# Work moved into the joints between stages, and the picking one-hot as one fused vector operation, in a two-layer graph network kernel

## The reference, cut to what matters

```python
h = relu(layernorm(x))
agg = segment_sum(h[src] * edge_weight[:, None], dst)       # over incoming edges
x = x + agg @ W_neigh + b_neigh + h @ W_self.T
h = relu(layernorm(x))                                      # not used by the second layer's result
s, m, c = segment_sum(attr, src), segment_max(attr, src), count(src)
u = [s, where(c > 0, m, 0), s / max(c, 1), u0]
x = x + relu(u @ W1 + b1) @ W2 + b2
```

## Time and profile before

| | us |
|---|---|
| median of 3 runs | 1644.15 |
| lowest, highest | 1643.24, 1649.29 |
| the profiled execution | 1640.22 |
| its span, first to last instruction | 1638.5 |
| busy in the span: PE, DVE, ACT, POOL | 986.9, 1323.9, 727.7, 1254.9 |

### The profile page before, as it was taken

How to read it: one execution, slowest core, us unless ns; L and a number is a source line. 1 busy time by engine, 2 the same in 40 slices (tenths; PEclk the granted TensorE clock), 3 DMA queues, 4 the chain that set the end, 5 groups by cost and what they waited for, 6 DMA issues and landing times. The chain is left out here.

```text
span 1638.5 us, 39257 instructions
## 1 busy us (share of the span) xinstructions
PE 986.9 (60%) x13658; PEld 839.9 (51%) x13659; DVE 1323.9 (81%) x3122; ACT 727.7 (44%) x1864; POOL 1254.9 (77%) x1506
## 2 busy tenths in 40 slices
PE   3356666666656102333333333359999999999995
PEld 2245555555555101323332233348878888888884
DVE  6689999999999104766766775659999999999995
ACT  2268888888874001221222222214444444444442
POOL 7777777776777777777777777458888888888882
PEclk9567787887876555555565555559999999999998
DMA  9955555555554103444434332259999999999996
GB/s 300 162 125 125 117 117 125 122 126 117 117 117 117 35 14 85 118 114 108 108 99 105 98 81 75 88 141 195 208 205 212 208 208 210 207 208 210 205 210 62
DMA packets 507051, 229.55 MB, mean 140 GB/s; under 512 B 472141, under 2 KB 479565, under 8 KB 506173
## 3 DMA queue, kind: packets, MB, share of 16 engines
q0 software_dynamic: 148560, 98.39, 36.4%
q1 hardware_dynamic: 356558, 118.63, 33.8%
q10 hardware_dynamic: 1728, 9.94, 1.5%
HBM read 138.46 MB, written 88.33 MB: 138 GB/s over the span
## 5 line engine op out<-in xcount | busy, mean ns | idle before, releaser
L851 POOL DMA_INDIRECT xg_all<-in_x_dram,idx_src x391 | 397.0, 1015 | 120.2 <-issue 118.5
L857 POOL DMA_INDIRECT by_win<-rows,idx_win x391 | 389.4, 996 | 130.1 <-issue 129.5
L1186 PE MATMUL ps<-ident,h 128*128 128x128 f32 x588 | 138.1, 380 | 283.4 <-DVE h L1000 207.6
L1272 ACT ACTIVATE sq<-xc 128x512 f32<-128x512 f32 x147 | 92.6, 630 | 474.6 <-DVE xc L963 473.0
L1186 PEld LDWEIGHTS ps<-ident,h 128*128 128x128 f32 x588 | 93.4, 196 | 303.0 <-DVE h L1000 220.7
L952 DVE TENSOR_REDUCE stat<-xg_all 128x8 f32<-128x512 f32 x49 | 33.4, 682 | 233.0 <-DMA xg_all<-in_x_dram,idx_src 232.9
L1414 POOL DMA_DIRECT2D rows<-flag_d x392 | 197.0, 539 | 3.5 <-issue 3.5
L1290 ACT ACTIVATE h<-xc,stat 128x64 f32<-128x64 f32 x784 | 196.2, 332 | 0.0
L1425 POOL DMA_DIRECT2D out_dram<-rows x97 | 162.6, 1676 | 28.6 <-ACT rows L1616 21.7
L1570 PE MATMUL ps<-w_sb,arena 128*96 128x64 f32 x1568 | 156.5, 254 | 0.0
L1570 PEld LDWEIGHTS ps<-w_sb,arena 128*96 128x96 f32 x1568 | 142.9, 167 | 22.7 <-issue 22.7
(11 more groups left out here) (212 smaller groups left out, 2635.9 us busy)
## 6 DMA issues: line engine op xcount, KB each, us to landing
rows<-message SPq DMA_DIRECT2D x784, 36.4 KB, 3.6
rows<-flag_d POOLq DMA_DIRECT2D x392, 72.0 KB, 4.2
out_dram<-rows POOLq DMA_DIRECT2D x97, 256.0 KB, 6.2
message<-m_row SPq DMA_DIRECT2D x48, 388.0 KB, 2.4
arena<-in_x_dram SPq DMA_DIRECT2D x70, 256.0 KB, 3.6
out_dram<-arena SPq DMA_DIRECT2D x70, 256.0 KB, 2.9
zeros<-slot_d POOLq DMA_DIRECT2D x98, 144.0 KB, 4.1
by_win<-zeros ACTq DMA_DIRECT2D x12, 808.5 KB
```

The source lines that it names most:

```text
L851: nc.gpsimd.indirect_dma_start(out=xg[g % RX][:, t % GT, :], out_offset=None, in_=x, in_offset=bass.IndirectOffsetOnAxis(ap=idx_src[:, t:t ...
L857: nc.gpsimd.indirect_dma_start(out=by_win, out_offset=bass.IndirectOffsetOnAxis(ap=idx_win[0:parts, t:t + 1], axis=0), in_=rows[0:parts, t ...
L1186: last = nc.tensor.transpose(hT_of[n % 2][:, P * k:P * k + P], h[n % 2][:, 2 * k:2 * k + 2, :].rearrange("p a c -> p (a c)"), ident[:, :])
L1272: nc.scalar.activation(sq[:, :, :], xc[n % 2][:, :, :], ACT.Square).then_inc(ln["squared"], 1)
```

## The change

Its parts:

- *Start.* SP issues the main src load first, ahead of its wait for the pads. POOL clears only the columns from FT on of five tables. Gathers of full tiles read `src_i` directly; `idx_src` is one column, for the tail tile, and POOL waits for it only before the gathers of group 8 on.
- *First block, tail.* DVE makes the bias rows after edge steps 10 and 11, the counts after 12. After the last gather POOL makes a table `node_n`, 8 x 128 columns with 0 to 1023, and issues the loads of window groups 0 to 3. The last steps have an order of their own: DVE keeps the steps up to LAST-2 before it sums the last one.
- *Window block.* The loads of groups 0 to 3, the bias rows and PE's wait for them are gone. `picks` is one scalar_tensor_tensor: (key - 1024 g) == node_n.
- *Last block.* The counts are gone.

The tiles of the window block are laid out anew: loads, pick, node_n and the bias rows in `rows`, the rest in `arena`.

```diff
-        idx_src = sb("idx_src", [P, NT], U32)
+        idx_src = sb("idx_src", [P, 1], U32)
...
+                sp.dma_start(src_i[:, 0:FT], src[0:FT * P].rearrange("(p t) -> p t", p=P)).then_inc(loaded["src"], 16)
                 sp.wait_ge(made["pads"], 1)
-                edge_load(sp, src_i, src, "src")
+                sp.dma_start(src_i[0:TAIL, FT:FT + 1], src[FT * P:E].rearrange("(p o) -> p o", o=1)).then_inc(src_tail, 16)
...
-                nc.gpsimd.memset(src_i[:, :], -1)
-                nc.gpsimd.memset(dst_i[:, :], -1)
-                nc.gpsimd.memset(code_i[:, :], -1)
-                nc.gpsimd.memset(next_i[:, :], N)
-                nc.gpsimd.memset(ew[:, :], 0.0)
+                nc.gpsimd.memset(src_i[:, FT:], -1)
+                nc.gpsimd.memset(dst_i[:, FT:], -1)
+                nc.gpsimd.memset(code_i[:, FT:], -1)
+                nc.gpsimd.memset(next_i[:, FT:], N)
+                nc.gpsimd.memset(ew[:, FT:], 0.0)
...
-                            in_offset=bass.IndirectOffsetOnAxis(ap=idx_src[:, t:t + 1], axis=0)).then_inc(x_here[g % RX], 16)
+                            in_offset=bass.IndirectOffsetOnAxis(ap=(src_i[:, t:t + 1].bitcast(U32) if t < FT else idx_src[:, 0:1]),
+                                                                axis=0)).then_inc(x_here[g % RX], 16)
...
-                pool.wait_ge(made["srcs"], 1)
+                pool.wait_ge(loaded["src"], 16)
                 for g in range(EARLY):
                     gather(g)
...
+                pool.wait_ge(made["srcs"], 1)
                 for g in range(EARLY, MG):
                     gather(g)
                 pool.wait_ge(win_sent, 16 * (FT + 1))
+                own(nc.gpsimd.iota(node_n[:, :, :], [[P, GT], [1, P]], base=0, channel_multiplier=0,
+                                   allow_small_or_imprecise_dtypes=True))
+                pool.wait_ge(order_out[0], 64)
+                for g in range(RING):
+                    load_group(pool, g)
...
-                dve.wait_ge(loaded["src"], 32)
-                own(nc.vector.tensor_scalar(idx_src[:, :], src_i[:, 0:NT], 0.0, None, ALU.max))
-                dve.sem_inc(made["srcs"], 1)
+                dve.wait_ge(loaded["src"], 16)
+                dve.wait_ge(src_tail, 16)
+                nc.vector.tensor_scalar(idx_src[:, :], src_i[:, FT:FT + 1], 0.0, None, ALU.max).then_inc(made["srcs"], 1)
...
+                LAST = len(steps) - 1
                 sort = iter(())
                 for kind, g in tail_steps:
                     n = step_of[kind, g]
+                    if n == LAST:
+                        continue
...
+                    if kind == "edge" and g == SORT_AT[0] + 1:
+                        dve.wait_ge(win_sent, 16 * (FT + 1))
+                        c0_rows()
+                    if kind == "edge" and g == SORT_AT[0] + 2:
+                        bias_row()
+                    if kind == "edge" and g == SORT_AT[0] + 3:
+                        longest_count()
-                scale_of(len(steps), 1)
-                weigh(len(steps) - 1)
-                relu_of(len(steps) - 1)
-                for n in range(len(steps) - LAG, len(steps)):
-                    keep(n, 0)
-                    keep_left(n)
-                    keep_middle(n)
-                    keep_low(n)
+                scale_of(LAST, 1)
+                weigh(LAST - 1)
+                kept_of(LAST - LAG)
+                relu_of(LAST - 1)
+                kept_of(LAST - 3)
+                kept_of(LAST - 2)
+                sums_of(LAST)
+                centre(LAST)
+                spread_of(LAST)
+                scale_of(LAST + 1, 1)
+                weigh(LAST)
+                relu_of(LAST)
+                kept_of(LAST - 1)
+                kept_of(LAST)
...
-                for n in range(len(steps), len(steps) + 3):
-                    if n - 2 < len(steps):
-                        turn(n - 2)
-                    project(n - 3)
+                turn(LAST - 1)
+                project(LAST - 2)
+                project(LAST - 1)
+                turn(LAST)
+                project(LAST)
...
-                for st in tail_steps:
+                for st in tail_steps[:-1]:
                     step(step_of[st])
-                relu(len(steps) - 1)
-                turned(len(steps) - 2)
-                turned(len(steps) - 1)
+                relu(LAST - 1)
+                turned(LAST - 2)
+                turned(LAST - 1)
+                square(LAST)
+                root(LAST)
+                turned(LAST)
...
-                    own(nc.vector.tensor_tensor(near[c][:, :], chunk[b][0:CH, :, KEY], first_of[0:CH, g * GT:g * GT + GT],
-                                                ALU.subtract))
-                    nc.vector.tensor_tensor(pick[c][0:CH, :, :], iota_n[0:CH, :].unsqueeze(1).to_broadcast([CH, GT, P]),
-                                            near[c][:, :].unsqueeze(2).to_broadcast([CH, GT, P]),
-                                            ALU.is_equal).then_inc(w["pick"], 1)
+                    nc.vector.scalar_tensor_tensor(pick[c][0:CH, :, :], chunk[b][0:CH, :, KEY].unsqueeze(2).to_broadcast([CH, GT, P]),
+                                                   float(g * GT * P), node_n[0:CH, :, :],
+                                                   ALU.subtract, ALU.is_equal).then_inc(w["pick"], 1)
...
-                own(nc.vector.tensor_tensor(counts[:, 0, :], starts[:, 0, 1:NW + 1], starts[:, 0, 0:NW], ALU.subtract))
-                own(nc.vector.tensor_copy(counts[:, 1, :], starts[:, 1, 0:NW]))
-                own(nc.vector.tensor_reduce(longest[:, :], counts[:, :, :].rearrange("p n l -> p (n l)"), AX, ALU.max))
```

More of the change, by code:

```diff
@@ L688, in last_nodes, with in_rows @@
             return (table[WF * GT * P:(WF * GT + WR) * P, :].rearrange("(k p) c -> p k c", p=P), table[N - N % P:N, :])
+        RING = 4
+        flat = rows[:, :, :].rearrange("p t c -> p (t c)")
+        def in_rows(at, k, c):
+            return flat[:, at:at + k * c].rearrange("p (k c) -> p k c", k=k)
+        XW, CW, AW, FW = GT * D, GT * RM, GT * RE, 2 * 3 * SL
+        KC = CH + 1
+        y = [in_rows(b * XW, GT, D) for b in range(RING)]
+        chunk = [in_rows(RING * XW + b * CW, GT, RM) for b in range(RING)]
@@ new lines, in part_of @@
+        def part_of(tile, parts, *shape):
+            size = math.prod(shape)
+            at = taken[0]
+            taken[0] += size
+            piece = tile[0:parts, at:at + size]
+            if len(shape) == 1:
+                return piece
+            return piece.rearrange("p (k c) -> p k c", k=shape[0])
+        pick = [part_of(flat, P, GT * P // 2).bitcast(BF16).rearrange("p (k c) -> p k c", k=GT) for _ in range(2)]
+        c0_row = part_of(flat, P, GT * D // 2).bitcast(BF16).rearrange("p (k c) -> p k c", k=GT)
@@ new lines, in graph_layers @@
+        c0_one = part_of(flat, P, SL // 2).bitcast(BF16)
+        c0_sum = part_of(flat, P, D)
+        bias_left = part_of(flat, P, D)
+        node_n = part_of(flat, P, GT, P)
+        bias_part = part_of(flat, P, KEY).bitcast(BF16).rearrange("p (n c) -> p n c", n=PARTS)
+        assert taken[0] <= NT * RE
+        taken[0] = 0
+        perm = part_of(arena, SL, GT * SL)
+        sums, tops, means = (part_of(arena, P, 2 * SL) for _ in range(3))
+        hid = part_of(arena, P, GT * SL)
+        v_left = part_of(arena, SL, GT, D)
@@ new lines, in graph_layers @@
+        v_part = [parts_of(part_of(arena, SL, GT, KEY)) for _ in range(2)]
+        sel = [part_of(arena, SL, GT * P // 2).bitcast(BF16).rearrange("p (k c) -> p k c", k=GT) for _ in range(2)]
+        assert taken[0] <= 2 * SB * RE
+        o_bank, pp_bank, z_bank, v_bank = (0, 1), 3, (4, 5, 6, 7), 2
+        z_all = ps_all[:, 4 * 512:8 * 512].rearrange("p (q c) -> p q c", c=512)
+        zq_ps = z_all[:, :, 0:2 * SL]
+        w = {n: sem(f"win_{n}") for n in ("perm", "pp", "u", "z", "hid", "v_ps", "high",
+                                          "left", "mid", "v", "sel", "pick", "picked", "o_ps", "y")}
@@ new lines, in bias_row @@
+                def bias_row():
+                    own(nc.vector.tensor_copy(bias_part[:, 0, :], biasb[:, :]))
+                    own(nc.vector.tensor_tensor(bias_left[:, :], biasb[:, :], bias_part[:, 0, :], ALU.subtract))
+                    own(nc.vector.tensor_copy(bias_part[:, 1, :], bias_left[:, :]))
+                    own(nc.vector.tensor_tensor(bias_part[:, 2, :], bias_left[:, :], bias_part[:, 1, :], ALU.subtract))
+                    for c in range(2):
+                        own(nc.vector.memset(pick[c][CH:KC, :, :], 1.0))
+                    for b in range(RING):
+                        own(nc.vector.tensor_copy(chunk_p[b][CH:KC, :, :, :],
+                                                  bias_part[CH:KC, :, :].unsqueeze(1).to_broadcast([1, GT, PARTS, D])))
@@ new lines, in longest_count, with kept_of @@
+                def longest_count():
```

(23 more changed lines are left out.)

119 lines of the change are left out of this document (42 added, 77 removed).

## The result

| | before | changed |
|---|---|---|
| median of 9 runs, us | 1640.06 | 1631.65 |
| lowest, highest, us | 1636.93, 1649.29 | 1626.34, 1637.26 |
| the profiled execution, its span, us | 1640.22, 1638.5 | 1631.32, 1629.6 |

The ratio is 0.9945 with a 95% interval of [0.9925, 0.9965]: 8 to 9 us less, where 37 were forecast. The forecast, 1607, and its range are missed by far. The sum was made against one profiled execution, and so is the account of the miss.

The account below looks back on a forecast made before the run. POOL's indirect DMAs bound the first part to 1047.8 us, then a joint, then DVE to 1613. Gains 2.6 + 0.8 + 12.7 + 17.6 + 3.35 = 37.05 took 1640.2 to 1603.2, 1607 as median; range 1598 to 1618.

Parts of the forecast that it names:

- the picking one-hot: Window stage: one fused operation replaces subtraction, wait and compare, saving 0.185 us in each of 95 groups, 17.6 us.
- joints: Kernel start and the passage from first block to window stage: forecast to gain 16.1 us together.
- Start: Kernel start: less clearing and a shorter wait for indices bring the first gather forward, 2.6 us gained, bounds 1 to 3.
- Work in the holes: First block's edge steps 10 to 12: bias rows and counts, 12.2 us, fit into VectorE's waits at cost 0.
- Last edge group: First block's end: keeping three earlier steps before the last sum gains 0.8 us, between +1 and -3 on time.
- Loads moved ahead: First block's end: POOL's table and 24 window loads behind the last gather cost 0, at most 2 us.
- Start of the window stage: From the block change to group 1's hidden products: 12.0 us instead of 24.7, gaining 12.7, bounds 10 to 15.
- rival D: Last stage: fused operation takes two cycles an element, 1.08 us more per group, 106 us, total 1713; chance 0.03.
- End: Last block: the counts leave it, where they were the chain, gaining 3.35 us.
- Rival B: Window stage: TensorE with ScalarE, or the transfers, hold the period at 5.36 us, total 1624.6; chance 0.10.
- C: Joints give half: early loads delay stores or TensorE's clock stays low three or four groups longer, total 1617; chance 0.08.
- E: Last stage: TensorE stays at 1.2 GHz, 2.6 us per further group, 1685 at 30 groups; chance 0.02.

Follow-up runs that it names:

- e1: Changed kernel with the old subtraction, wait and compare for picking: 1960.07 us, ratio 0.9946 to the kernel before; period 5.513 us.
- e2: Kernel before with only the fused one-hot added, its table made at the window block's start: 1974.64 us, ratio 1.0036 to the kernel before; period 5.446 us.
- e6: Kernel before with two of the eight message loads per group issued by ScalarE: 1638.68 us, ratio 0.9996 to the kernel before; period 5.384 us.
- e7: Kernel before with the fused one-hot and two message loads per group on ScalarE: 1622.34 us, ratio 0.9905 to the kernel before; period 5.220 us.
- e15: Changed kernel with two of the eight message loads per group on ScalarE: 1934.81 us, ratio 0.9809 to the kernel before; period 5.227 us.
- e14: Changed kernel without the adding of finished groups to out: 1951.51 us in one run, beside 1970.33 for the kernel before; period 5.444 us.
- e4: Changed kernel with each message load bringing 48 rows instead of 96, same number of issues: 1951.96 us, ratio 0.9913 to the kernel before; period 5.39 us.
- e8: Changed kernel with a ninth SP load of 128 bytes per group: 1693.58 us, ratio 1.0327 to the kernel before; period 6.119 us.
- e9: Changed kernel unaltered, run again with a longer first block: 1927.16 us, ratio 0.9998 to the kernel before; period 5.443 us.
- e10: Changed kernel with the old picking pair, run again: 1924.5 us, ratio 0.9995 to the kernel before; period 5.510 us.
- e11: Changed kernel with two of eight message loads per group on ScalarE, an earlier run: 1896.4 us, ratio 0.9828 to the kernel before; period 5.189 us.
- e12: Changed kernel with three of eight message loads per group on ScalarE: 1905.33 us, ratio 0.9884 to the kernel before; period 5.238 us.

## Why the prediction was wrong

**The step that failed** is the last sentence on the picking one-hot: "SP issues 8 x 0.53 = 4.3 us and a register load: both stay under 5.17." I took the pace of SP from a mean over its first 16 issues, 8.55 us, in which no long issue fell: between 1066.0 and 1090.3 us no 16 KB instruction packet moved. Over a whole group SP needs 5.34 to 5.6 us. In the kernel before it went almost exactly as fast as VectorE and lived on a lead (landing to picking: in the mean 7.9 us in groups 4 to 16, 5.1 up to group 60, 4.3 in the last ten), so VectorE never waited for it. The question that I left out: what SP itself waits for. Waits of SP in the window stage of before:

```profile
SPq L1399 <- PE ps L1581: 10.7, 6, 5.9
```

These six are groups 4 to 9, while SP was four groups ahead. After them its first issue came some 3 us after the release of the buffer, so the 5.40 us at which it then went (groups 16 to 97) was its own pace, with next to nothing in hand against the 5.38 of VectorE.

**The other half of that error** is that the changed joints take the lead away. I costed the bias rows' move as a plain gain; but the 8.9 us of VectorE at the stage's start were also what put SP ahead. With no lead SP's pace becomes the period at once. How high that pace is, is another thing, and open: in groups 16 to 97 SP took 5.40 and 5.39 us a group in the two traces of the kernel before, 5.49 and 5.46 in those of the changed one, 5.53 in e1 and e2. So the lost lead explains that the period follows SP, and not that it is 0.10 longer than before instead of merely no shorter.

Point by point:

- *Start*: forecast 2.6 us; the first gather came 1.95 us earlier (12.42 to 10.47, not near 9.8: POOL still idled 0.99 us in front of it, not 0.3), the last 3.2, just past the bound of 3. Right in the main; the 1.2 us between the two came from nothing that was forecast.
- *Work in the holes*: cost 0, right; DVE's waits for rows fell by 22 us, not 12.
- *Last edge group*: forecast a gain of 0.8, found a loss of 1.1 (3.2 less 2.1), just outside the bound of 1. The last sum came 1.25 us later, not 3, but less was won behind it. The prediction has no term for the cast that ran 1.36 us longer beside the new IOTA; without it the order would have been worth some 0.3.
- *Loads moved ahead*: forecast 0 with a bound of 2, found 1.9. POOL's issues were done at 1058.2, even before the 1061 to 1063 forecast, and delayed no store (the last landed 2.9 us after its issue, as before). What was not in the sum is POOL's DRAIN of 7.90 us behind them: it, and no longer SP's last store, set the block's end.
- *Start of the window stage*: forecast 12.7, found 14.1 from the change of blocks on. Right, inside the bound of 15, with the wait in the forecast place.
- *The picking one-hot*: the operation is as fast as forecast (1215 ns against 1222), so rival D is out; what the pair costs more is shown by e6 and e7, 0.164 us a group, where the forecast was 0.185. By the Trainium skill ("VectorE: DVE Perf Modes", The DRAIN you can't avoid) it was to be no more than 0.15; the measurement lies between the two. All of it was hidden behind SP: 26.4 us of error in a sum that missed by 28.1, the other 1.8 being the joints (14.3 for 16.1, in which errors of both signs partly cancel: some luck).
- *End*: 3.35, right.
- *Rival B*, "the period doesn't shrink", came true in its outcome and not in its cause. It named TensorE with ScalarE and the transfers; e7 and e15 exclude both, at more products and more bytes per us. Its time, 1624.6, was also too low: it had the period unchanged, not 0.10 us longer, and the joints 1.8 us too good. It had a chance of 0.10 since "DVE waits for no load there": true, and no evidence, as a queue that keeps up from a lead makes no wait.
- *Rivals C, D, E*: not seen. The granted clock was 1.00 from 1090 us on (before, 0.64 in 1100 to 1105), and the fused operation took 1215 ns. Of C's early loads, no store was delayed, but POOL's DRAIN behind them took the 1.9 us above, far from the 10 of C.

## What to carry to other kernels

Before shortening the engine that is the bound, work out the pace of every queue that feeds it from its count over a long stretch (issues per us, long ones included), not from the duration of one issue or a burst, and compare that with the new period. A queue with no wait behind it may be living on a lead; a change that starts the consumer earlier spends that lead. Where a queue is within a few per cent, move a part of its issues to an idle one in the same change: here the fused operation was worth nothing, and 16 us once two loads of eight had moved.

## What the runs showed of the hardware that was not expected

- One in ten of SP's DMA issues takes 0.6 to 2.2 us instead of 0.317. Of these 1002 in 1093 begin while a 16 KB packet of the queue labelled "instruction" moves, against 319 in 10158 of the short ones, and they end 0.37 us after it (17 traces). It is the same without the stores of another queue (e14) and with half the bytes (e4).
- A VectorE cast of 128x512 f32 to bf16, 0.42 us in the median, took 1.79 and 1.80 us in the two traces in which POOL's IOTA of 128x1024 f32 (1.04 us) ran beside it (the changed kernel, e8). A tensor_tensor and a scalar_tensor_tensor beside the same IOTA kept their 0.69 us (e9, e10, e11, e12).
- Behind its last direct DMAs of the first block POOL's DRAIN takes 7.90 us in each of the 12 traces with the loads moved ahead. Where POOL came late (changed kernel, e8), the other engines waited for its end, 1.9 and 2.0 us; where the first block was longer, it was over before.
- A three-operand operation that reads a 1024-column f32 table beside a spread key takes 1215 ns, no more than the two-operand compare (1222).
- VectorE's own period differs by stretches: in e11 5.156 us in groups 22 to 71 and about 5.22 from 80 on, with VectorE never idle. The difference lies between the start of the permutation and that of value_left, 529 and 596 ns; not explained.
